# Second attention of a two-layer transformer block: scores computed twice, key-major tiles for the exponential, query maxima moved into rows by SBUF-to-SBUF transfers

## The reference, cut to what matters

```python
def _L1_cond_ref(x, c, g1, w_ada1, b_ada1, w_qkv, b_qkv, w_proj, ...):
    B, T, D = x.shape              # 4, 1024, 512
    H = 16
    hd = D // H                    # 32
    xn = adaln(x, c, g1, w_ada1, b_ada1)
    qkv = bitlinear(xn, w_qkv, b_qkv).reshape(B, T, 3, H, hd)
    q, k, v = (qkv[:, :, i].transpose(0, 2, 1, 3) for i in range(3))
    attn = jax.nn.softmax(jnp.einsum('bhqd,bhkd->bhqk', q, k) * hd ** (-0.5), axis=-1)
    o = jnp.einsum('bhqk,bhkd->bhqd', attn, v).transpose(0, 2, 1, 3).reshape(B, T, D)
    x = x + bitlinear(o, w_proj, b_proj)
    ...
```

## Time and profile before

| what | us |
|---|---|
| median of 3 runs | 4012.0 |
| the profiled execution, its own time | 4011.16 |
| its span | 4009.4 |
| second attention, from its first DMA issue to the first instruction of the next stage | 2547.6 to 3636.6 |
| PE busy in the span | 3775.5 (94%) |
| DVE, ACT, POOL busy in the span | 2721.6, 2687.9, 1035.5 |

### The profile page before, as it was taken

The page is one execution under the profiler, slowest core; times in us unless marked ns, Lnnn a source line. Parts: engine busy times, 40 slices in busy tenths (PEclk is TensorE's granted clock), DMA queues, the critical chain, the costliest instruction groups (busy, mean ns, idle before and its releaser), DMA issues. The chain is left out here.

```text
span 4009.4 us, 70221 instructions
## 1 busy us (share of the span) xinstructions
PE 3775.5 (94%) x26756; PEld 2543.0 (63%) x26756; DVE 2721.6 (68%) x4863; ACT 2687.9 (67%) x4667; POOL 1035.5 (26%) x1544
## 2 busy tenths in 40 slices
PE   8997999999999986999999959799999999995999
PEld 7885666666666664778888835466666666662555
DVE  4335888888888876444421148688888888885987
ACT  2226888888888854222222238688888888884998
POOL 0004555555555465000000037100000000002554
PEclk9998999999999998999999979899999999997999
DMA  5446233333333088244531038733332333313221
GB/s 189 184 164 152 62 67 62 67 62 67 62 67 62 14 285 272 100 137 158 176 114 53 32 131 303 205 62 67 62 67 62 67 61 67 62 30 127 77 80 51
DMA packets 307567, 419.53 MB, mean 105 GB/s; under 512 B 89449, under 2 KB 165741, under 8 KB 307227
## 3 DMA queue, kind: packets, MB, share of 16 engines
q1 hardware_dynamic: 307232, 415.03, 36.8%
HBM read 257.34 MB, written 157.32 MB: 103 GB/s over the span
## 5 line engine op out<-in xcount | busy, mean ns | idle before, releaser
L555 ACT ACTIVATE Sn<-Sn,mn 128x1024 f32<-128x1024 f32 x1024 | 1174.8, 1147 | 30.4 <-DVE mn L583 19.0
L521 PEld LDWEIGHTS pt<-ident,Sn 128*128 128x128 f32 x8192 | 881.2, 141 | 420.8 <-issue 413.5
L521 PE MATMUL pt<-ident,Sn 128*128 128x128 f32 x8192 | 1123.4, 280 | 1.0 <-DVE PT L547 0.4
L545 ACT ACTIVATE PT<-pt 128x512 f32<-128x512 f32 x1280 | 738.2, 597 | 236.0 <-PE pt L521 235.9
L489 PE MATMUL sp<-KS,QS 97*128 97x512 f32 (+1 forms) x2048 | 733.6, 440 | 45.3 <-DMA KS<-s_khi 23.6
L583 DVE CUSTOM_DVE_ANT_0 Sn<-sp,biastile 128x1024 f32<-128x1024 f32 x512 | 624.4, 1220 | 145.1 <-PE sp L489 113.5
L585 DVE TENSOR_SCALAR_CACHE_REDUCE Sn<-sp 128x1024 f32<-128x1024 f32 x512 | 624.3, 1220 | 137.3 <-PE sp L489 137.3
L628 POOL TENSOR_SCALAR biastile<-dist,ascale 128x1024 f32<-128x1024 f32 x512 | 576.3, 1126 | 497.0 <-DVE mn L583 483.9
L510 PE MATMUL po<-PT,Vp 128*32 128x256 f32 x8192 | 651.4, 391 | 0.0
L547 DVE COPY PT<-pt 128x512 f32<-128x512 f32 x768 | 531.2, 692 | 118.5 <-PE pt L521 118.3
L1077 ACT ACTIVATE gf<-pf,b1T 128x512 f32<-128x512 f32 x128 | 88.3, 690 | 535.4 <-PE pf L1022 530.5
(11 more groups left out here) (237 smaller groups left out, 4985.8 us busy)
## 6 DMA issues: line engine op xcount, KB each, us to landing
QS<-s_qhi SPq DMA_DIRECT2D x128, 256.0 KB, 5.0
KS<-s_khi SPq DMA_DIRECT2D x128, 256.0 KB, 7.2
KS<-s_klo SPq DMA_DIRECT2D x64, 256.0 KB, 6.1
QS<-s_qlo SPq DMA_DIRECT2D x64, 256.0 KB, 6.9
Vp<-s_v SPq DMA_DIRECT2D x64, 256.0 KB, 7.8
s_o<-og SPq DMA_DIRECT2D x32, 512.0 KB, 8.7
xA<-in_x SPq DMA_DIRECT2D x8, 1024.0 KB, 5.7
s_qhi<-qstage SPq DMA_DIRECT2D x32, 256.0 KB, 2.0
```

The lines of the kernel that those rows point to most:

```text
L521: op = nc.tensor.transpose(ps[:, i, :], sn[:, (g * HALF + i) * P:(g * HALF + i + 1) * P], K.ident[:])
L545: nc.scalar.activation(dst, src, ACT.Copy).then_inc(*s_cp_act.up())
L555: nc.scalar.activation(sn[:], sn[:], ACT.Exp, scale=-1.0, bias=mn[n % 3][:, t:t + 1], accum_out=sums[n % 5][:, t:t + 1]).then_inc(*s_exp.up())
```

## The change

The second attention gets a function of its own, `stage_attention1`; the first one is untouched. The line numbers of all that follows it rise by 234. In it each score is computed twice:

- `score` as before, in query-major tiles, but only for the minima: DVE reduces it with a plain `tensor_reduce` (`minimum`), and nothing is written but `mn`. Tile t of a head now holds every eighth query (`t:L:LT` as weights), so that `mn` on partition p holds the minima of queries 8p to 8p+7.
- `minima_halves` (POOL, two small instructions per head) splits `mn` into a high and a low half in fp32r, and `rows_to_queries` (SP, two DMAs per head) writes them from 128 partitions x 32 bytes into one row each, rows 96 and 97 of the `QS1` buffer. Rows 96 and 97 of `KS1` are set to -1.0 once.
- `score_turned` computes the scores again with the keys on the partitions, contracting over 98 rows, so that the minimum is already subtracted: 2 matmuls of 512 queries per block of 128 keys, each into one of two one-bank buffers `st1`. ACT takes the exponential straight from there into `PT1` (`exponential`, 128x512, two per tile).
- `times_v` is as before. The sums come from PE too: POOL adds two neighbouring key blocks of `PT1` (`add_pair`, 128x1024, two per four tiles), and `total` multiplies them by a matrix of ones in four column strips into `pz1`. DVE copies `po1` and `pz1` (`take_output`), `turn_output` has 4 transposes instead of 2, and `output` takes the reciprocal from the transposed sums.
- The transposes of the exponentials (`turn`) and their copies are gone.

The order is written in windows `w` of four tiles, that is half a head, 128 windows and 10 more. In window w PE computes the minima scores of tiles 4w to 4w+3, the turned scores of window w-4, and `times_v` and `total` of window w-5; `take_output` comes at w-7 and `turn_output` and `output` at w-8, in every second window.

```diff
+        def tensor_program():
+            for w in range(NW + TAIL):
+                for i in range(4):
+                    if 0 <= w - 4 < NW:
+                        score_turned(4 * (w - 4) + i, 0)
+                    if w < NW:
+                        score(4 * w + i, 0)
+                    if w < NW and i == 3:
+                        score(4 * w + i, 1)
+                    if 0 <= w - 4 < NW:
+                        score_turned(4 * (w - 4) + i, 1)
+                    if w < NW and i < 3:
+                        score(4 * w + i, 1)
+                n, odd = divmod(w - 8, 2)
+                if not odd and 0 <= n < N_HEADS:
+                    turn_output(n)
+                if 0 <= w - 5 < NW:
+                    for i in range(4):
+                        times_v(4 * (w - 5) + i)
+                    for i in range(2):
+                        total(2 * (w - 5) + i)
...
+        def score(u, g):
...
+            ps = ps_r.take(pe, u, (s_min, u + 1)) if g == 0 else ps_r.at[u]
+            nc.tensor.matmul(ps[:, g * BLK:(g + 1) * BLK], qs[0:ROWS, j, t:L:LT],
+                             ks[0:ROWS, j, g * BLK:(g + 1) * BLK], start=True, stop=True).then_inc(*s_score.up())
...
+        def score_turned(u, g):
...
+            pe.wait_ge(s_row[n % 2], 32 * (n // 2 + 1))
...
+            ps = pst_r.take(pe, ("st", u, g), (s_exp, 2 * u + g + 1))
+            nc.tensor.matmul(ps[:], ks_l.at[p][0][0:ROWS + 2, j, kb * P:(kb + 1) * P], qs_l.at[p][0][0:ROWS + 2, j, g * BLK:(g + 1) * BLK],
+                             start=True, stop=True).then_inc(*s_st.up())
...
+            nc.scalar.activation(pT[n % 2][:, kb, g * BLK:(g + 1) * BLK], pst_r.at["st", u, g][:], ACT.Exp, scale=-1.0).then_inc(*s_exp.up())
...
+            nc.vector.tensor_reduce(mn[n % 2][:, t:t + 1], ps_r.at[u][:], AX.X, ALU.min).then_inc(*s_min.up())
...
+                nc.sync.dma_start(qs_l.at[p][0][ROWS + half:ROWS + half + 1, j, :].bitcast(F32),
+                                  mm[n % 2][:, half, :].bitcast(F32)).then_inc(*s_row[n % 2].up(16))
...
+        def vector_program():
+            for w in range(NW + TAIL):
+                if w < NW:
+                    minimum(4 * w)
+                n, odd = divmod(w - 7, 2)
+                if not odd and 0 <= n < N_HEADS:
+                    take_output(n)
+                if w < NW:
+                    for i in range(1, 4):
+                        minimum(4 * w + i)
+                n, odd = divmod(w - 8, 2)
+                if not odd and 0 <= n < N_HEADS:
+                    output(n)
...
-        stage_attention(K, 1)
+        stage_attention1(K)
```

159 lines of the change are left out of this document (added).

## The result

The changed kernel is slightly slower. Its median is 4016.4 us (4012.8 to 4019.5, 20 runs) against 4010.9 us before (4006.0 to 4015.6, 20 runs) on the same chip: ratio 1.0015, interval 1.0008 to 1.0022. The profiled execution took 4017.4 us. The forecast was 3981, so sign and size are wrong; the time lies inside the range of 3935 to 4065.

What follows compares the result with a forecast made beforehand. PE was taken to bound the second attention. Fill 23.8, windows 5 to 7 23.6, 120 windows at 8.01 and the drain came to 1044 us against 1075.5: 31 less, 3981 us for the median, range 3935 to 4065.

Steps and rivals of the forecast that it cites:

- the ring of turned scores: Two buffers between PE's turned scores and ACT's exponentials: one turn takes 1.17 to 1.18 us.
- 0.04 until the other engine starts: In a buffer's turn, the time from the matmul's end to the exponential's start: 0.04 us.
- 0.39 + 0.09: In a buffer's turn, the turned score's matmul, 0.39 us, and its exposed weight load, 0.09 us.
- rival 2: Turned-score and minima-score buffers hold each other up on PE's queue: slower, 4004 with exponentials of 0.69, up to 4024; chance 0.20.
- The drain: Stage's end after the last scores: four windows 29.8 us, one with products only 3.2, last output 2.7.
- the fill: Stage's start, from the first score to the end of window 4: 23.8 us.
- The odd window: `take_output` between DVE's first two reductions delays tile 3's score to 4.45, products to 5.14; window 8.00 us.
- POOL's sums: Sums of two tiles of 128x1024, 2.5 to 2.7 us each, two per window, hidden.
- The rows: The minima's two DMAs per head: landing allowed 7.2 us, needed 13 us after, so hidden.
- The stepped load: Weight load of every eighth query for minima scores: taken as hidden beneath the matmul ahead, up to 0.23 us.
- over 0.3: Sign that the forecast is wrong: weight loads of the minima scores last over 0.3 us.
- the upper bound: Weight load of every eighth query at 0.43 us does not hide: 106 us more, 4087; chance 0.17.

Runs made afterwards that it cites:

- e9: Changed kernel with ACT waiting for the products and sums of the head before last once per head, not at each key block: 4001.3 us, ratio 0.9976.
- the filler: Changed kernel with matmuls nobody reads in the last four windows, where the minima scores would stand: 4012.9 us, ratio 1.0005.
- e2: Changed kernel with `take_output` ahead of a window's first reduction instead of behind it: 3992.5 us, ratio 0.9957.
- e6: Changed kernel with turned scores over 96 rows, without the minima's two rows or the wait for them: 4016.8 us, ratio 1.0015.
- e4: Changed kernel with minima scores reading 128 neighbouring queries instead of every eighth, so each query gets another's minimum: 4004.1 us, ratio 0.9985.
- e3: Changed kernel with three one-bank buffers each for turned and minima scores, and `take_output` ahead of the first reduction: 3944.3 us, ratio 0.9836.
- e12: Changed kernel with three buffers each, copies first, ACT's waits once per head, and neighbouring queries as weights with others' minima: 3929.1 us, ratio 0.9795.

## Why the prediction was wrong

**The step that failed** is the ring of turned scores, in its term "0.04 until the other engine starts". It was read from DVE behind PE in the kernel before, where a single wait stands in front of the reduction. The exponential of the changed kernel that opens a turn has two or three in front of it, and starts 0.10 to 0.12 us after the matmul. Three hundredths more came from the matmul itself, 0.51 with its load where 0.39 + 0.09 had been summed; this part is read from the rows and was not tested. Turns of 1.26 to 1.27 are the point from which, by the prediction, rival 2 decides ("a turn of 1.26 instead of 1.18"), and the time is in its band (4004 to 4024). Its cause is only half what the rival said: the exponential took 0.60, not 0.69, and the rings did not hold each other up. In even windows PE has no wait for DVE, and e9 alone, which touches only ACT's waits, brought back 1.19. The kernel before had the evidence in its trace: DVE's copy L547 starts 0.106 us after the transpose where a separate wait stands behind the release, and 0.037 where none does. I took one row for all.

**Two terms were mis-sized.** The drain was summed at full clock and ran at 0.67 in the profiled execution, +9.7. With the filler, at full clock, it took 37.8, so about 2 of the 9.7 are the longer turns and the rest is the clock; in the usual execution the clock costs some 4. In the fill PE ran at half clock until the first turned scores were done, and window 4 took 6.6 us (2576.2 to 2582.8) where the forecast had 3.2; DVE's reductions ahead of it gave half a microsecond back, together +2.9. The steady part carries most of it, 26.4 of 40.2. But the sign needed the ends as well: of the forecast gain of 31 us the steady part alone would have left some 5.

**What held.** The odd window: the wait for DVE behind `take_output` came where it was placed; the window was 8.09 for 8.00. The agreement is closer than its parts: the copies start 0.34 apart where 0.38 each was summed, and tile 3's score came at 4.34 instead of 4.45; behind it two stepped loads stood exposed, and the products started at 5.37 instead of 5.14; the products, 2.72 for 2.86, gave some back. e2 shows the mechanism. POOL's sums are hidden, at 2.375 each. The rows are hidden (e6), landing after 2.0 us where 7.2 was allowed. The clock stays at 1.00 in the steady part.

**The stepped load** was taken as hidden up to 0.23 and lasts 0.324; the prediction named "over 0.3" as a sign against itself. It costs 12 us (e4), not the 106 of the upper bound. Its length is not its pace: two of them in a row last 0.56 together, so the second starts 0.24 after the first. What is left exposed are mainly the two of odd windows. The Trainium skill says in "SBUF — State Buffer" (the note on cachelines) that a step over four fp32 values pays a penalty. The trace agrees in direction: 324 against 190 ns for the same count. For the exponential, the Trainium skill's rule in "ScalarE: Activation LUTs" (the rates of ACTIVATE), the same rate for every function and some 93 ns more for each per-partition operand, agrees too: without such an operand it took 0.595, as the copy before.

**Where the forecast gain went**: of 1.55 us per window that PE's work alone promised, 0.12 were left (8.35 before, 8.23 now). PE's three waits are 1.48 us per window (180 us in some 121.5), 0.35 more in even windows than worked out. e3 and e12 win part of it back, and their new bound is DVE's eight reductions in a burst.

## What to carry to other kernels

When a ring of two buffers sets the pace, its turn is a sum of row lengths and of two releases, and a release is dearer when further waits of the waiting instruction are still to be dealt with behind it; a wait that is always long satisfied still cost 0.06 to 0.08 us on such a path here, and is better made once per outer loop. Look also at the ends: a deeper pipeline pays for its fill and drain, here more than the steady part won. Put what is left of the last item of work (here two copies) where its engine idles, not between two links of the current chain. Where a forecast's gain is below 1% and slack in it below 0.1 us, check its prices on every form of the same event in the trace, not on one row.

## What the runs showed of the hardware

- From the matmul's end to the start of ACT: 0.038 us with one semaphore wait in front, 0.097 with two, 0.119 with three (541 cases). The further waits cost this where their own instruction stands behind the release; where it was over before (270 cases with two waits in the kernel before), the start is at 0.037 to 0.038. For PE's load behind ACT it is 0.05.
- A weight load of 128 columns from every eighth fp32 value lasts 324 ns, from neighbouring ones 190; two stepped ones in a row start 0.24 us apart.
- In the drain, PE busy 27.42 of 30 us with a pause in each turn of the ring, the granted clock was 0.67; with filler matmuls, busy 28.63, it was 1.00.
- A transfer of 128 pieces from SBUF to one row in SBUF lands after 2.0 us with 4 KB and 2.1 with 0.5 KB; the 16 issues take 10.3 us on SP.
